# A graph network on one core: SyncE issues the sums of both blocks of a pair ahead of its wait for the pair's mask buffer

## What is computed

```python
total = jnp.concatenate([atom_fea[dst], atom_fea[src], edge_fea], axis=1)
total = _batchnorm(total @ fc_w.T + fc_b, bn1_w, bn1_b)
gate, core = jnp.split(total, 2, axis=1)
messages = jax.nn.sigmoid(gate) * jax.nn.softplus(core)
aggr = jax.ops.segment_sum(messages, dst, num_segments=N)
```

## Time and profile before

| | |
|---|---|
| median of 3 runs | 10983.7 us (10974.28 to 10992.69) |
| profiled execution, its time | 10998.39 us |
| its span | 10996.7 us |
| first and last affine instruction of the message pass | 5729.7 and 6551.5 us from the span's start |
| busy over the span | PE 58%, VectorE (DVE) 52%, ScalarE (ACT) 29%, POOL 64% |

### The profile page before, as it was taken

The page is one execution under the profiler, slowest core; times in us unless marked ns, Lnnn a source line. Parts: engine busy times, 40 slices in busy tenths (PEclk is TensorE's granted clock), DMA queues, the critical chain, the costliest instruction groups (busy, mean ns, idle before and its releaser), DMA issues. The chain is left out here.

```text
span 10996.7 us, 138229 instructions
## 1 busy us (share of the span) xinstructions
PE 6379.7 (58%) x42657; PEld 5452.4 (50%) x42755; DVE 5713.8 (52%) x8038; ACT 3161.8 (29%) x4908; POOL 6995.6 (64%) x6971
## 2 busy tenths in 40 slices
PE   3666666548888566666653333455555455555553
PEld 2555555437788555445431113454544445555453
DVE  3555555689951655555557764333333443333335
ACT  1333333227710011111117761222222222222221
POOL 4777777715500577777764444777777767777774
PEclk9888888769999888888875556777777777777776
DMA  7666666514457477777765542444444334444442
GB/s 126 188 195 192 195 190 193 162 67 183 194 193 279 149 234 235 237 239 233 235 198 187 187 162 66 126 122 126 124 126 122 103 102 124 124 124 124 126 122 72
DMA packets 1299105, 1783.39 MB, mean 162 GB/s; under 512 B 619145, under 2 KB 794044, under 8 KB 1289322
## 3 DMA queue, kind: packets, MB, share of 16 engines
q1 hardware_dynamic: 816519, 882.68, 24.9%
q10 hardware_dynamic: 269696, 616.64, 15.2%
q0 software_dynamic: 212704, 281.43, 11.4%
HBM read 922.11 MB, written 857.87 MB: 162 GB/s over the span
## 5 line engine op out<-in xcount | busy, mean ns | idle before, releaser
L615 POOL DMA_INDIRECT arena<-table_d,idx_src x3136 | 2963.6, 945 | 1121.5 <-issue 955.3
L759 PE MATMUL pn<-work,wblk 128*128 128x128 f32 x3136 | 959.3, 405 | 1887.7 <-DMA arena<-table_d,idx_src 1887.7
L615 POOL DMA_INDIRECT arena<-in_x_dram,idx_src x1568 | 1523.7, 972 | 591.4 <-issue 477.0
L615 POOL DMA_INDIRECT arena<-tsrc_d,idx_src x1568 | 1482.1, 945 | 478.0 <-issue 478.0
L1329 DVE TENSOR_SCALAR idx_src<-src_all 128x8 int32 (+1 forms) x784 | 139.5, 179 | 3124.0 <-PE pn L760 2392.9
L759 PEld LDWEIGHTS pn<-work,wblk 128*128 128x128 f32 x3136 | 755.2, 296 | 1963.5 <-DMA arena<-table_d,idx_src 1005.9
L760 PE MATMUL pn<-ident,arena 128*128 128x128 f32 x4704 | 1292.6, 371 | 0.0
L1071 ACT ACTIVATE arena<-pn 128x512 f32<-128x512 f32 x1470 | 793.0, 594 | 1274.1 <-PE pn L791 1167.1
L760 PEld LDWEIGHTS pn<-ident,arena 128*128 128x128 f32 x4704 | 1096.6, 286 | 0.0
L749 PE MATMUL pn<-work,weT 128*128 128x512 f32 x784 | 553.9, 796 | 663.7 <-DMA arena<-tsrc_d,idx_src 635.8
L1376 DVE TENSOR_TENSOR_SCAN work<-keep,work,pn 128x512 f32<-128x512 bf16 x588 | 752.7, 1280 | 274.4 <-PE ph L772 203.0
(11 more groups left out here) (364 smaller groups left out, 13511.0 us busy)
## 6 DMA issues: line engine op xcount, KB each, us to landing
runs_d<-arena ACTq DMA_DIRECT2D x588, 768.0 KB
adj_d<-feat SPq DMA_DIRECT2D x37, 3136.0 KB, 10.7
feat<-adj_d SPq DMA_DIRECT2D x37, 3136.0 KB, 10.9
seed_d<-nothing SPq DMA_DIRECT2D x392, 256.0 KB
arena<-seed_d SPq DMA_DIRECT2D x392, 256.0 KB, 6.8
attr<-in_edge_attr_dram SPq DMA_DIRECT2D x392, 256.0 KB
feat<-total_d SPq DMA_DIRECT2D x196, 512.0 KB
keep<-keep_d SPq DMA_DIRECT2D x588, 128.0 KB
```

Source lines behind the costliest of these rows:

```text
L615: g.indirect_dma_start(out=to, out_offset=None, in_=table, in_offset=bass.IndirectOffsetOnAxis(ap=idx, axis=0))\
L759: mm(to, wblk[:, PNA.index(p), j, :], feat_to[u], start=True, stop=False, skip_group_check=True)
```

## The change

In SyncE's loop of the message pass the loads are issued at even u only: the sums of block u, the sums of block u + 1, and then the wait for the pair's mask buffer and the mask. Before, the order was sums u, mask (with its wait), sums u + 1. The number of DMAs and their sizes stay the same, and so do the first iteration's loads and all other engines' programs.

```diff
                     with sp.Fori(1, IT) as i:
                         for u in range(U):
                             if p == MSG:
-                                attr_load(p, i, u)
-                                mask_load(p, i, u)
+                                if u % 2 == 0:
+                                    attr_load(p, i, u)
+                                    attr_load(p, i, u + 1)
+                                    mask_load(p, i, u)
                             elif p == SOFT:
                                 attr_load(p, i, u)
                                 mask_load(p, i, u)
```

## The result

The changed kernel takes 10918.8 us (median of 5 runs, 10912.0 to 10937.6), the kernel before 10982.0 us (median of 5), a ratio of 0.9948 with a 95% interval of 0.9934 to 0.9962: 63 us less. The forecast was 10924 us, 60 us less, with a range of 10900 to 10958.

A forecast was written before the change was run, and what follows sets the result against it. Late loads, passed through POOL and VectorE, were taken to hold ScalarE below its limit. The profiled 10998.4 us, less 69 gained, plus 10 contention, gave 10939; for the median 10924 us, range 10900 to 10958.

The forecast's parts named there:

- Which load is late: SyncE's load(n+1), behind the mask's wait for scan(n-3), misses its cap by 0.7 us; load(n+2) just arrives.
- The margins: After the change, sums leave POOL ahead of their caps by 3.2 us for block n, 4.3 us for block n+1.
- The next limit: With the delay gone, ScalarE sets the message pass's pace at 3.86 us a block; VectorE needs 3.5 us.
- What it returns: Gain in the message pass from removing each pair's delay: 70 us by pace, 68 us by waits, taken as 69 us.
- Contention, 10 us: POOL halves and VectorE's softplus maximum delay each other: some 40 cases, 10 us lost, bounds 0 and 24 us.
- the marker: Sign of contention in the changed profile: a mean of VectorE's maxima above 0.80 us means the charge was too low.
- The price of 0.25 us: Cost charged per stretched VectorE maximum: with one of 1.18 us the copy-to-copy step is 4.00 us, not 3.75.
- The mask: The mask's issue at scan(n-3) stays, the loads queued ahead are out of its way, so the cost is nothing.
- More contention: Rival: POOL delays VectorE's maximum and cap, 25 us above forecast, 10949 us (22 to 45 less than before); chance 0.19.
- POOL waits for loads about as often: Sign in the changed profile: POOL still waits for loads about as often as before, but a block ahead of need.
- the rule's estimate of 14 us: Shared-port rule: a maximum meets a POOL half in 40% of blocks, losing some 0.07 us a block, 14 us.

The follow-up runs named there:

- e2: Changed kernel with the mask and its wait ahead of both loads of the pair; 11244.1 us, ratio 1.0242 to the kernel before.
- e3: Changed kernel with the next pair's loads issued ahead of the mask's wait, so no load waits for a scan; 10913.8 us, ratio 0.9940 to the kernel before.
- e5: Changed kernel with the gate's Exp over 256 of 512 columns, half the gate not computed; 10900.2 us, stretch 724.6 us.
- r0: The changed kernel itself, run again beside e4, e5 and e6; 10904.8 us, ratio 0.9920 to the kernel before, stretch 753.6 us.
- e4: Changed kernel with POOL's affine instructions over 256 of 512 columns, half the scaled sums not computed; 10899.8 us, stretch 746.5 us.
- e9: e6 with the load order of the kernel before; 13350.1 us beside 13355.7 us for the kernel before, ratio 1.0001.
- e11: e10 with the next pair's loads issued ahead of the mask's wait, as in e3; 10786.5 us, ratio 0.9821 to the kernel before.
- e6: Changed kernel with the pass's output DMAs issued by SyncE instead of ScalarE, nothing left out; 10873.1 us, ratio 0.9895 to the kernel before.
- e8: e6 with POOL's affine instructions over 256 of 512 columns; 13250.2 us beside 13355.7 us for the kernel before, ratio 0.9918.
- e10: e6 with VectorE capping block n+2 before the maximum of block n+1; 13221.2 us beside 13355.7 us for the kernel before, ratio 0.9899.

## Why the prediction was right

- *Which load is late, and that its lateness is all of it.* Right. One late load per pair, handed on to POOL, cap and Exp; after the change both waits are gone, and e2 and e3 show that less lead costs 258 us of the stretch and more gives nothing.
- *The margins.* Wide enough, as forecast, but not the 3.2 us of block n: 2.5 to 2.6. POOL starts on it 4.4 and 4.9 us after the end of scan(n-5), near the 4.5 charged, but its two halves take some 2.5 us beside VectorE, in place of up to 2.0. Block n+1 has 4.2 and 5.3 us, forecast 4.3.
- *The next limit, ScalarE at 3.86 us a block.* Right: 3.85 us, and e5 shows that it is ScalarE. VectorE's work, forecast at 3.5 us, is 3.65, still below.
- *What it returns, 69 us.* Right to a few us: the stretch fell by 65.5 us with the added contention in it (63.5 in r0), and with half of the affine work away, in e4, by 70.6. The 69 us before contention can't be measured alone.
- *Contention, 10 us.* The time came out (59 us forecast as the net gain, 63 measured), but the marker did not hold and the charge was too high. The maxima's mean went to 868 and 942 ns, above the 800 named, but the cost did not follow: if the 69 us hold, 3.5 to 5.5 us more than in the kernel before. The price of 0.25 us for a stretched maximum, from one block of the earlier trace rows, was charged for each, but maxima of 0.86 to 0.88 us in the iteration above stand in steps of 3.75 to 3.81 us.
- *The mask.* Right: no wait for it appears.
- *More contention as a rival.* Its mechanism is real, the cap can be hit (up to 1107 ns, median 680), its price is not: the stretch shortened by 65.5 us, above the 45 that bounded this case.
- *POOL waits for loads about as often.* Wrong: 95 times for 140. Both loads of a pair are in when it starts, so it does four halves in a row.

What the prediction saw too small is the structure. It counted delays against ScalarE's limit; the kernel before was a closed loop, and 0.6 us a block taken from ScalarE did not help it (e9). And its view of what comes behind ended at ScalarE's 3.86 us.

The Trainium skill (SBUF — State Buffer, section "SBUF: two separate sides") names VectorE instructions with two SBUF inputs or in a two-port mode as those that GpSimd can block. The traces agree in kind: maximum, product and cap reach 1150, 1196 and 1107 ns, while the scan, with one input from PSUM, keeps a mean of 1271 to 1279 ns in every run. As a count of lost time the rule's estimate of 14 us was too high here, because most of a block's delay falls into VectorE's slack.

## What to carry to other kernels

When an in-order queue issues loads behind a wait for something else, follow the wait round: if it closes a loop through the loads (scan, load, affine, cap, scan), the loop's length over the blocks that it covers is the pace, and making the busiest engine faster changes nothing. Move whatever does not need the wait ahead of it, up to the margin that the timeline shows; more lead is worth nothing until the next limit falls, and then it is worth checking again (e3 gave 0, the same edit in e11 came with 74 us). Read the delay for each position in the unrolled iteration by itself, since equal-looking pairs can differ by a factor of two, as they did here (45.2 against 19.9 us).

## What the runs showed of the hardware

- An output DMA on the engine that computed it costs that engine 0.60 us a block here (a wait for its own copy's end, then the issue), and 0.97 us at the turn of the loop; on SyncE it cost none of it.
- POOL's and VectorE's delays depend on which starts first. In all 14 traces no maximum, product or cap that starts with no POOL half running takes more than 724 ns, even where a half starts inside it; the longer ones start while a half runs. And a half that starts inside a cap does not get in ahead of the maximum that follows without a gap: 208 such maxima in e10 and e11 took 685 ns on average and 698 at most, while the 190 in r0 that start out of an idle time with a half running took 943.
- At the turn of the hardware loop, once in four blocks, ScalarE's gap behind the copy is 0.97 us in place of 0.60, but only where ScalarE issues the store: in e6 and e8 to e11 it has no gap there at all. VectorE's gap ahead of the product is 0.21 us there in place of 0.09, in every run.
